# A second table buffer, and constant rows set from ScalarE's queue, in a disentangled-attention kernel

## The reference

```python
scores = jnp.einsum('bhqd,bhkd->bhqk', q, k) / scale
pos_k = (rel_embeddings @ Wk + bk)...                       # 128 buckets
c2p = take_along_axis(einsum('bhqd,hpd->bhqp', q, pos_k), c2p_pos)   # per distance q - k
p2c = take_along_axis(einsum('bhkd,hpd->bhkp', k, pos_k), p2c_pos)
scores = scores + (c2p + swapaxes(p2c, -1, -2)) / scale
ctx = softmax(scores) @ v
```

## Time and profile before

| | us |
|---|---|
| median of 3 runs (lowest, highest) | 2065.32 (2064.91, 2070.2) |
| the profiled execution's own time | 2074.24 |
| its span, first to last instruction | 2072.4 |
| TensorE busy over the span | 1716.4 (83%) |
| VectorE busy | 1358.2 (66%) |
| ScalarE busy | 1071.2 (52%) |
| GpSimd busy | 1071.1 (52%) |
| DMA, mean rate over the span | 225 GB/s |

### The profile page before, as it was taken

How to read it: one execution, slowest core, us unless ns; L and a number is a source line. 1 busy time by engine, 2 the same in 40 slices (tenths; PEclk the granted TensorE clock), 3 DMA queues, 4 the chain that set the end, 5 groups by cost and what they waited for, 6 DMA issues and landing times. The chain is left out here.

```text
span 2072.4 us, 40517 instructions
## 1 busy us (share of the span) xinstructions
PE 1716.4 (83%) x13688; PEld 1153.3 (56%) x13688; DVE 1358.2 (66%) x3937; ACT 1071.2 (52%) x2169; POOL 1071.1 (52%) x1265
## 2 busy tenths in 40 slices
PE   1981159999989899999999999999993566799997
PEld 1440035555555555555555555655552455799996
DVE  1662058789888788888788887888872464243333
ACT  1662136666667566666666666666661461122221
POOL 0210067677766667667576676766740450233332
PEclk9996569999999999999999999999996575899999
DMA  3697378777777877777877777777736961677772
GB/s 117 190 303 245 108 241 265 246 261 251 244 254 257 253 251 245 258 251 259 254 250 257 250 261 248 251 257 254 240 105 154 289 208 36 227 213 221 217 221 81
DMA packets 327354, 465.95 MB, mean 225 GB/s; under 512 B 35516, under 2 KB 260687, under 8 KB 327054
## 3 DMA queue, kind: packets, MB, share of 16 engines
q1 hardware_dynamic: 314814, 428.09, 64.7%
q10 hardware_dynamic: 7344, 20.84, 3.3%
q0 software_dynamic: 4992, 14.43, 1.9%
HBM read 269.90 MB, written 193.65 MB: 224 GB/s over the span
## 5 line engine op out<-in xcount | busy, mean ns | idle before, releaser
L864 ACT ACTIVATE t_probsT<-t_flip 128x512 f32<-128x512 f32 x1024 | 611.5, 607 | 245.2 <-PE t_flip L762 128.0
L816 DVE TENSOR_REDUCE t_most<-t_scores 128x1 f32<-128x640 f32 (+1 forms) x512 | 437.2, 854 | 263.9 <-PE t_scores L739 257.9
L858 ACT COPY t_table<-t_table_ps 128x512 f32<-128x512 f32 x512 | 299.2, 584 | 227.7 <-DMA skew_d<-t_table 138.2
L835 DVE TENSOR_SCALAR t_band<-t_band,t_top 128x384 f32<-128x384 f32 (+1 forms) x512 | 367.6, 718 | 0.0
L912 POOL TENSOR_TENSOR t_near<-t_near,t_masks 128x384 f32<-128x384 f32 (+1 forms) x128 | 147.2, 1150 | 371.6 <-DMA t_near<-skew_d 370.9
L776 PE MATMUL t_sum_ps<-t_probsT,t_vals 128*32 128x256 f32 x4096 | 330.9, 395 | 0.2 <-ACT t_probsT L864 0.2
L718 PE MATMUL t_table_ps<-t_rows,t_quest 96*128 96x256 bf16 x512 | 144.8, 283 | 176.3 <-ACT t_table L858 89.6
L928 POOL TENSOR_TENSOR t_near<-t_near,t_masks 128x768 f32<-128x768 f32 (+1 forms) x128 | 273.1, 2134 | 0.0
L762 PE MATMUL t_flip<-t_masks,t_band 128*128 128x128 f32 x1408 | 262.2, 275 | 0.0
L820 DVE CUSTOM_DVE_ANT_0 t_band<-t_scores,t_near 128x384 f32<-128x384 f32 (+1 forms) x512 | 262.1, 512 | 0.0
L732 PE MATMUL t_scores<-t_after,t_quest 105*128 105x256 bf16 (+3 forms) x1024 | 246.7, 291 | 0.0
(11 more groups left out here) (181 smaller groups left out, 2373.7 us busy)
## 6 DMA issues: line engine op xcount, KB each, us to landing
skew_d<-t_table SPq DMA_DIRECT2D x128, 1024.0 KB, 9.0
t_near<-skew_d SPq DMA_DIRECT2D x128, 640.0 KB, 6.0
t_near<-skew_d SPq DMA_DIRECT2D x128, 384.0 KB, 4.9
e_w<-in_L_ffn_W_dram ACTq DMA_DIRECT2D x39, 512.0 KB, 4.2
e_w<-in_L_ffn_W_dram SPq DMA_DIRECT2D x39, 512.0 KB, 4.0
split_d<-p_part SPq DMA_DIRECT2D x32, 384.0 KB
t_after<-split_d SPq DMA_DIRECT2D x64, 192.0 KB
t_quest<-split_d SPq DMA_DIRECT2D x64, 192.0 KB
```

Of the source, the lines that this page charges most:

```text
L816: nc.vector.tensor_reduce(most[:, c, 1:2], out[:, wide:S], AX.X, ALU.max)
L835: nc.vector.tensor_scalar(band[n % 2][:, t, 0:wide], band[n % 2][:, t, 0:wide], top[n % 2][:, t:t + 1], None, ALU.subtract).then_inc(level ...
L858: nc.scalar.copy(table[:, h, :, u % 4, :], table_ps[:, :, :]).then_inc(table_kept, 1)
L864: nc.scalar.activation(probsT[s % 3][:, half * 512:(half + 1) * 512], flip_ps[half][:, :], ACT.Exp, scale=SCALE).then_inc(expd, 1)
```

## The change

- `table` becomes a list of two buffers, one for even and one for odd units; ScalarE's guard now looks at the write of two units before.
- The stacks' extra rows are put in another order, so that the constant rows of `after` and of `before` are nine neighbours (FAR to ROWS). Two tiles, `after_rows` (VectorE) and `before_rows` (GpSimd), are set to the nine rows' pattern by three memsets each.
- SP's 42 transfers are gone. ScalarE issues eighteen ahead of its loop, three for each buffer.
- SP issues `rows` first of all; the masks come after the loads of unit 0.
- TensorE no longer waits ahead of its loop for the masks, the bf16 identity and all constant rows: it waits for the first two at score 0 and for each buffer's constant rows at the first score of its unit.

```diff
-        table = sb("table", [P, 2, 2, 4, SPOT])
+        table = [sb(f"table{i}", [P, 2, 2, 4, SPOT]) for i in range(2)]
...
-            sp.dma_start(masks[:, :, :], c_masks).then_inc(const_in, 16)
-            sp.wait_ge(set_up, 3)
-            for i in range(BUFS):
-                sp.dma_start(quest[i][KROWS + 6:XROWS, :], ones[0:3, :]).then_inc(rows_set, 16)
-                sp.dma_start(after[i][MROW:ROWS, :], minus[0:3, :]).then_inc(rows_set, 16)
-                sp.dma_start(before[i][MROW:ROWS, :], minus[0:3, :]).then_inc(rows_set, 16)
-                sp.dma_start(after[i][KROWS:KROWS + 3, :], zeros[0:3, :]).then_inc(rows_set, 16)
-                sp.dma_start(after[i][KROWS + 3:KROWS + 6, :], ones[0:3, :]).then_inc(rows_set, 16)
-                sp.dma_start(before[i][KROWS:KROWS + 3, :], ones[0:3, :]).then_inc(rows_set, 16)
-                sp.dma_start(before[i][KROWS + 3:KROWS + 6, :], zeros[0:3, :]).then_inc(rows_set, 16)
+            sp.dma_start(rows[:, :, :, :].rearrange("p h a v -> p (h a v)"), pick_d[:, :]).then_inc(rows_in, 16)
...
                 if u == -4:
-                    sp.dma_start(rows[:, :, :, :].rearrange("p h a v -> p (h a v)"), pick_d[:, :]).then_inc(rows_in, 16)
+                    sp.dma_start(masks[:, :, :], c_masks).then_inc(const_in, 16)
...
@@ score(s), TensorE
+                if s == 0:
+                    pe.wait_ge(const_in, 16)
+                    pe.wait_ge(ident_made, 1)
+                if t == 0 and n < BUFS:
+                    pe.wait_ge(rows_set[n], 16 * 3)
...
-            pe.wait_ge(const_in, 16)
             pe.wait_ge(rows_in, 16)
-            pe.wait_ge(rows_set, 16 * 7 * BUFS)
-            pe.wait_ge(set_up, 4)
...
@@ VectorE
             nc.vector.memset(ones[:, :], 1.0).then_inc(set_up, 1)
-            nc.vector.memset(minus[:, :], -1.0).then_inc(set_up, 1)
-            nc.vector.memset(zeros[:, :], 0.0).then_inc(set_up, 1)
+            nc.vector.memset(after_rows[:, :], -1.0).then_inc(set_up, 1)
+            dve.wait_ge(set_up, 2)
+            nc.vector.memset(after_rows[0:6, :], 1.0).then_inc(set_up, 1)
+            dve.wait_ge(set_up, 3)
+            nc.vector.memset(after_rows[0:3, :], 0.0).then_inc(set_up, 1)
...
@@ keep_table(x), ScalarE
-                if u % 4 == 0 and n >= 1:
-                    act.wait_ge(skew_out[(n - 1) % 2][h], 16 * ((n - 1) // 2 + 1))
-                    act.wait_ge(side_kept, (n - 1) * 2 + h + 1)
-                nc.scalar.copy(table[:, h, :, u % 4, :], table_ps[:, :, :]).then_inc(table_kept, 1)
+                if u % 4 == 0 and n >= 2:
+                    act.wait_ge(skew_out[n % 2][h], 16 * (n // 2))
+                    act.wait_ge(side_kept, (n - 2) * 2 + h + 1)
+                nc.scalar.copy(table[n % 2][:, h, :, u % 4, :], table_ps[:, :, :]).then_inc(table_kept, 1)
...
@@ ScalarE, ahead of its loop
+            act.wait_ge(set_up, 4)
+            act.wait_ge(before_set, 3)
+            for i in range(BUFS):
+                for dst, src in ((quest[i][KROWS:FAR, :], ones[0:3, :]), (after[i][FAR:ROWS, :], after_rows[:, :]),
+                                 (before[i][FAR:ROWS, :], before_rows[:, :])):
+                    nc.scalar.dma_start(dst, src).then_inc(rows_set[i], 16)
...
@@ GpSimd, ahead of its loop
+            nc.gpsimd.memset(before_rows[:, :], -1.0).then_inc(before_set, 1)
+            pool.wait_ge(before_set, 1)
+            nc.gpsimd.memset(before_rows[0:6, :], 0.0).then_inc(before_set, 1)
+            pool.wait_ge(before_set, 2)
+            nc.gpsimd.memset(before_rows[0:3, :], 1.0).then_inc(before_set, 1)
```

More of the change, by code:

```diff
@@ L581, in attend @@
         ident16 = sb("ident16", [P, P], BF16)
-        ones, minus, zeros = (sb(w, [9, S], BF16) for w in ("ones", "minus", "zeros"))
+        ones, after_rows, before_rows = (sb(w, [9, S], BF16) for w in ("ones", "after_rows", "before_rows"))
         quest, after, before = ([sb(f"{w}{i}", [ROWS, S], BF16) for i in range(BUFS)] for w in ("quest", "after", "before"))
@@ L600, in attend @@
         sum_ps = ps("sum_ps", [P, 512])
-        const_in, rows_in, set_up, rows_set = sem("t_const_in"), sem("t_rows_in"), sem("t_set_up"), sem("t_rows_set")
+        const_in, rows_in, set_up = sem("t_const_in"), sem("t_rows_in"), sem("t_set_up")
+        before_set, ident_made = sem("t_before_set"), sem("t_ident_made")
+        rows_set = [sem(f"t_rows_set{i}") for i in range(BUFS)]
         hats_in = [sem(f"t_hats_in{i}") for i in range(BUFS)]
@@ L635, in load_unit @@
                                  ).then_inc(hats_in[i], 16)
-                for dst, far_at, many in ((quest[i][KROWS:KROWS + 6, :], n * (2 * far), 2 * PARTS),
-                                          (after[i][KROWS + 6:XROWS, :], (N + n) * (2 * far) + far, PARTS),
-                                          (before[i][KROWS + 6:XROWS, :], (N + n) * (2 * far), PARTS)):
+                for dst, far_at, many in ((quest[i][FAR:FAR + 6, :], n * (2 * far), 2 * PARTS),
+                                          (after[i][KROWS:FAR, :], (N + n) * (2 * far) + far, PARTS),
+                                          (before[i][KROWS:FAR, :], (N + n) * (2 * far), PARTS)):
                     sp.dma_start(dst, view(far_d, far_at, [[S, many], [1, S]])).then_inc(hats_in[i], 16)
@@ L652, in skew_write @@
                 sp.dma_start(view(skew_d, n % 2 * (P * PITCH) + h * 4 * SPOT + 1, [[PITCH, P], [TABLE, 2], [1, 4 * SPOT]]),
-                             table[:, h, :, :, :].rearrange("p a u v -> p a (u v)")).then_inc(skew_out[n % 2][h], 16)
+                             table[n % 2][:, h, :, :, :].rearrange("p a u v -> p a (u v)")).then_inc(skew_out[n % 2][h], 16)
             def skew_read(n, h):
@@ L838, in _ @@
             nc.vector.memset(ones[:, :], 1.0).then_inc(set_up, 1)
-            nc.vector.memset(minus[:, :], -1.0).then_inc(set_up, 1)
-            nc.vector.memset(zeros[:, :], 0.0).then_inc(set_up, 1)
+            nc.vector.memset(after_rows[:, :], -1.0).then_inc(set_up, 1)
[3 more added lines that the diff above has]
+            nc.vector.memset(after_rows[0:3, :], 0.0).then_inc(set_up, 1)
             dve.wait_ge(const_in, 16)
-            nc.vector.tensor_copy(ident16[:, :], masks[:, 4, :]).then_inc(set_up, 1)
+            nc.vector.tensor_copy(ident16[:, :], masks[:, 4, :]).then_inc(ident_made, 1)
             for s in range(TS):
@@ L899, in keep_side @@
                     pool.wait_ge(edge_made, (n - 2) * 10 + (5 if h == 0 else 10))
-                nc.gpsimd.tensor_copy(side[n % 2][:, :, 4 * h:4 * h + 4], table[:, h, :, :, BAND]).then_inc(side_kept, 1)
+                nc.gpsimd.tensor_copy(side[n % 2][:, :, 4 * h:4 * h + 4], table[n % 2][:, h, :, :, BAND]).then_inc(side_kept, 1)
             def edge(n, h, step):
```

1 line of the change is left out of this document (added).

## The result

The changed kernel has a median of 2043.98 us in 4 runs (2037.23 to 2049.48) beside 2065.11 for the kernel before: a ratio of 0.9891, with a 95% interval of 0.9857 to 0.9925. A later set of runs, in which the kernel before has a median of 2075.76, gave 0.9889 (0.9863 to 0.9914). The change is worth 21 to 23 us. The forecast was 31.9 us and 2033.4 us; the measured median lies in its range of 2021 to 2046, near the upper end, and outside the 2029 to 2041 that it gave to the forecast as built.

A forecast was written before the change was run, and what follows sets the result against it. The prediction took SP's closed ring of write, landing and reads to set the pace of `attend`. From the profiled 2074.24 us, - 30.8 - 1.5 + 0.4 gave 2042.3; carrying 8.9 over to the median gave 2033.4, range 2021 to 2046.

The forecast's parts named there:

- the forecast as built: The summed forecast for the whole kernel without the rivals, 2029 to 2041 us, held at 84 in 100.
- The bound: In `attend`, SP's write, landing, reads and next write set the pace, 9.91 us a half; compute engines' waits are slack.
- The start: At the start of `attend`, the first table copy comes at 216.3 in place of 247.11, a gain of 30.8 us.
- ScalarE's issues: Eighteen transfers ahead of ScalarE's loop in `attend` take 13.1 us from 203.2, freeing ScalarE at 216.3.
- `rows` and unit 0's loads: At the start of `attend`, both landed by about 213.5, so TensorE's first table matmul could start 33.0 us earlier.
- The second buffer: In `attend`, two table buffers remove ScalarE's wait and gain 1.5 us from late tables, between 0 and 5.0.
- the ring gets slower: Rival: earlier unit loads and stores or the new buffer's place lengthen SP's landings by over 8 us; 8 in 100.
- The new wait: In `attend`, TensorE would stand once in each unit for `near` (`near_made`), 1.5 to 2 us, instead of at the table.
- The tail: At the end of `attend`, TensorE's lead is worth nothing, since SP's last read already sets the tail.
- The carry to the median: The profiled execution's 8.9 us above the runs' median is carried over: 2042.3 becomes 2033.4 us.
- The table wait on the path: Rival: TensorE's 59.7 us of waiting for table copies in `attend` goes too, giving 1975 us; 6 in 100.
- Slow issues on ScalarE: Rival: at the start of `attend`, eighteen issues at 5.91 us each beside full DMA engines, giving 2128 us; 2 in 100.

The follow-up runs named there:

- table_only: The kernel before with the second table buffer alone: 2075.06 us beside 2075.76, ratio 0.9999.
- ahead_one: The changed kernel with SP issuing the write of a unit's second half before waiting for the first half's landing and reading it: 1932.69 us, ratio 0.9325.
- start_split: The changed kernel with head 0's rows loaded first, the other heads' after unit 0's loads, and ScalarE's transfers spread over the first steps: 2047.51 us, ratio 0.9871.
- setup_only: The changed kernel with one table buffer and the earlier guard, so only the new start: 2047.7 us, ratio 0.9863; repeated, 2050.25 us, ratio 0.9881.
- turn_late: The changed kernel with the transposition of the row maxima, and ScalarE's copy of it, one step later: 2055.82 us, ratio 0.991.

## Why the prediction was right, and where its terms were off

**The bound.** Right: the pace of the stage is SP's closed ring, and ScalarE's and TensorE's waits are slack. `table_only` removes ScalarE's wait and gains nothing, `ahead_one` opens the ring and gains some 117 us more than the change. The Trainium skill (Trainium Kernel Development and Optimization, section Best Practices) asks for double buffering; in this kernel the row `ACT t_table <- DMA skew_d<-t_table: 109.9` looked like its case, and a ratio of 0.9999 says that it wasn't.

**The start.** Right in kind, too large in size. The term was 30.8 us; it measures 28.2 to the first write in the first pair of profiles (27.7 to 28.5 over the other profiles with this start, against 52.4, the mean of the two of before). Two items made it up. ScalarE's issues: 13.1 us predicted, 14.9 measured, of which 1.57 for the first and 0.73 to 0.79 for the others, with gaps of 0.03; but they started after 3.8 us, where 4.2 had been allowed. (The 13.1 was called the middle of 12.4 and 14.0, which is 13.2.) `rows` and unit 0's loads: 14.5 us after the stage's start predicted, 19.3 measured. `rows` itself came sooner than predicted: the 12.5 us that it was given were 9.2. The step that failed is that unit 0's loads "have landed by about then as well": they had a term for their issue (3.5 us) and none for their landing, and they were complete some 8 us after `rows`. `start_split` shows the same with only 96 KB of `rows` in front: they landed in 2.0 us, and TensorE still started only 12.5 us after the stage's start, released by unit 0's loads. The Trainium skill (DMA: Bandwidth & Descriptors, section "Issuing engines are not separate DMA queues") calls issue time usually small beside the transfer; the trace disagrees here, as the issues of 42 small transfers alone stood for 28.9 us, and `setup_only`, whose new start is by the estimate above mainly their removal, gains 25 to 28 us.

**The second buffer.** The term was a gain of 1.5 us, with bounds of 0 and 5.0. Measured: nothing (`table_only`), perhaps a loss of 1 to 5 us. The step that failed is "the 5.0 us of late tables, which a lead of 1.46 us covers". SP's waits for tables (320 to 1460 us) rose to between 10 and 14 us in all five profiles that have the second buffer and the old order of SP; the two of `setup_only` have 3.0 and 3.1. TensorE is now held for the ring at L783 or L738, where the next tables stand behind it in its queue; that this is the cause is likely, not shown. That two thirds of such a delay come back by sooner landings was read from one landing of 10.15 and one of 9.38 us, among landings of 6.1 to 11.1; no run shows it. The rival "the ring gets slower" may hold a small share of this, and stays open.

**The new wait.** It came, in size (69.7 us for 59.7), at another line. The prediction followed `near_made` and overlooked that GpSimd's `split_top` stands behind the same read in GpSimd's queue and is wanted sooner. `turn_late` shows both places, one behind the other.

**The tail.** Right: 57.2 us from the last write to the next stage, as before (57.0).

**The carry to the median.** The forecast was summed against a profile of 2074.24 and carried over with the difference of 8.9 us. The pair of profiles moved by 30.7 (31.9 forecast), the medians by 21: the changed kernel's profile, 2043.53, stood at its own median and not 8.9 above. That the sum comes within 1.2 us of the profile is luck: the start gave 2.6 us less than forecast and the ring 2.4 less, and 3.6 us came from stages that the change hardly touches. The medians' 21 to 23 us are 5 to 7 short of the start's 28; on average of two profiles each, the ring of the changed kernel is 3 us longer, and the rest is open. Executions of the kernel before spread over 6 to 16 us in one set of runs, and that sets how well a sum of this kind can hit. The hit itself rests on the 12.7 us that the range allowed for landings.

**The rivals.** The table wait on the path: refuted by `table_only`. Slow issues on ScalarE: refuted in the changed kernel's own rows; while SP's issue at 204.04 took 7.94 us, ScalarE's went on at 0.73 to 0.79.

## What to carry to other kernels

Before a wait of a compute engine is given a price, look at the queue whose transfer it waits for: if that queue waits for the landings of its own transfers in nearly every row and for nothing else, it is a closed ring, and buffers at other engines only move their waits. Such a ring is opened by the order of the issues (the next write ahead of the wait for the last), here some 117 us for two exchanged calls; one more exchange lost it all again. Here transfers issued ahead of a stage's first operation counted in full; when they are cut, the data that TensorE waits for last sets the start. Ask for the landing of each of them, not only for its issue.

## What the runs showed of the hardware

- A queue of transfers can be held while another isn't: in the changed kernel, behind `rows` (landed by 208.1) and with `vals` under way, SP's issue of a 96-row load at 204.04 took 7.94 us, and in the same microseconds ScalarE's issues of 3 and 9 rows took 0.73 to 0.79 us.
- The same first write of 1 MB landed after 6.09 us in the changed kernel, and after 10.02 us in `start_split`, where unit 1's loads, behind the other heads' rows, were still under way.
- A memset of 1024 bf16 columns on GpSimd took 0.94 us for 9, 6 and 3 partitions alike.
